# Seventeen products per context piece, five transfers for g, the selected context and v2, and an earlier Wout load

## The reference

```python
query = hidden_states @ Wq                      # 100 x 640 for each batch
keyt, valt = enc @ Wk, enc @ Wv                 # 718 x 640
hs = _mha(query, keyt, valt)                    # softmax(q k^T / sqrt(80)) v, 8 heads
ca_q1 = einsum('btc,th->bch', ca, Wq_ca)[:, indices, :]
ca_hs1 = _mha(ca_q1, residual, residual)
ca_hs2 = _mha(ca_hs1 @ Wq, ca @ Wk_ca, ca @ Wv_ca)
out = (hs + ca_hs2) @ Wout + b_out + residual
```

## Time and profile before

| what | value |
|---|---|
| three runs | 996.71, 997.91, 1003.1 us; median 997.91 |
| the profiled execution | 995.0 us, its span 993.3 us |
| granted TensorE clock, mean | 0.997 |
| busy: TensorE, VectorE, ScalarE, GpSimd | 978.8, 649.9, 489.7, 342.4 us |
| DMA | 190.12 MB, 191 GB/s |

### The profile page before, as it was taken

One profiled execution on the slowest core, in us unless ns is written; L12 is line 12 of the kernel. 1 busy time (PEld: TensorE's weight loads), 2 busy tenths in 40 slices (PEclk: granted clock), 3 DMA queues, 4 the chain that ended last, 5 costly groups with the idle time before them and its releaser, 6 DMA issues.

```text
span 993.3 us, 20727 instructions
## 1 busy us (share of the span) xinstructions
PE 978.8 (99%) x6740; PEld 959.5 (97%) x6740; DVE 649.9 (65%) x1129; ACT 489.7 (49%) x895; POOL 342.4 (34%) x286
## 2 busy tenths in 40 slices
PE   9999999999999999999999999999999999998998
PEld 8998889999999999999999999999999999997997
DVE  6455686767666666666766767676767666667444
ACT  7434546464545455454646463636364645445120
POOL 5212453333343434251616152434333333415000
PEclk9999999999999999999999999999999999999999
DMA  7899978887878787978797979697878878795364
GB/s 263 279 296 268 267 172 203 173 206 158 205 170 197 168 196 167 197 172 188 174 186 180 183 182 185 179 184 192 171 199 169 209 155 209 166 211 149 99 186 144
DMA packets 154170, 190.12 MB, mean 191 GB/s; under 512 B 80929, under 2 KB 108193, under 8 KB 154145
## 3 DMA queue, kind: packets, MB, share of 16 engines
q1 hardware_dynamic: 147456, 177.44, 76.2%
q10 hardware_dynamic: 6688, 12.35, 3.8%
HBM read 81.56 MB, written 19.95 MB: 102 GB/s over the span
## 4 chain that ended last, share of the span: by engine, by line
PE 88%; DVE 4%; DMA 3%; ACT 2%; SPq 2%; issue 1%; ACTq 0%
PE psS L744 22%; PE psB L779 20%; PE psB L784 10%; PE psS L719 8%; PE psT L760 6%; PE psS L888 6%; PE psT L806 4%; PE psT L812 2%; PE psB L923 2%; PE psS L997 1%; PE psB L861 1%; PE psB L838 1%; PE psT L813 1%; DMA encT_raw<-in_Wout_dram 1%; SPq L382 1%; PE psB L849 1%
## 5 line engine op out<-in xcount | busy, mean ns | idle before, releaser
L744 PE MATMUL psS<-encT_keep,Wk_keep 128*128 128x360 f32 x1440 | 253.8, 329 | 0.0
L744 PEld LDWEIGHTS psS<-encT_keep,Wk_keep 128*128 128x128 f32 x1440 | 237.4, 189 | 0.8
L779 PE MATMUL psB<-PT_h,encN_h 120*128 120x400 f32 x576 | 202.6, 352 | 0.0
L779 PE MATMUL psB<-PT_l,encN_h 120*128 120x400 f32 x576 | 199.0, 345 | 0.0
L1130 ACT ACTIVATE probs<-psS,negmax 100x718 f32<-100x718 f32 x128 | 110.2, 861 | 130.7 <-DVE negmax L1522 130.6
L606 POOL TENSOR_TENSOR encT_keep<-encT_raw,encT_keep 128x718 fp32r<-128x718 f32 x45 | 79.7, 1771 | 179.9 <-ACT encT_keep L1159 177.6
L1535 DVE TENSOR_TENSOR PT_l<-psT,PT_h 120x600 fp32r<-120x600 f32 x128 | 99.7, 779 | 43.3 <-ACT PT_h L1141 39.2
L614 POOL TENSOR_TENSOR encN_l<-enc_raw,encN_h 120x768 fp32r<-120x768 f32 x48 | 92.6, 1929 | 92.5 <-ACT encN_h L1166 91.1
L784 PE MATMUL psB<-PT_h,encN_l 120*128 120x400 f32 x576 | 120.4, 344 | 0.7 <-POOL encN_l L614 0.7
L597 POOL TENSOR_TENSOR Mbd<-Mbd,fmask 128x320 fp32r<-128x320 f32 x48 | 45.0, 937 | 220.6 <-DMA Mbd<-m_split 218.1
L1546 DVE TENSOR_TENSOR kT<-psS,kT 128x718 fp32r<-128x718 f32 x80 | 72.3, 903 | 69.4 <-ACT kT L1154 69.4
(11 more groups left out here) (245 smaller groups left out, 1630.1 us busy)
## 6 DMA issues: line engine op xcount, KB each, us to landing
kstack<-kT SPq DMA_DIRECT2D x64, 448.8 KB
kstack<-kT SPq DMA_DIRECT2D x192, 112.2 KB
enc_raw<-in_encN_dram SPq DMA_DIRECT2D x48, 360.0 KB, 5.5
encT_raw<-in_encT_dram SPq DMA_DIRECT2D x45, 359.0 KB, 6.2
kstack<-kT SPq DMA_DIRECT2D x32, 359.0 KB
kstack<-kT SPq DMA_DIRECT2D x32, 269.2 KB
kstack<-kT SPq DMA_DIRECT2D x32, 179.5 KB, 3.7
kstack<-kT SPq DMA_DIRECT2D x64, 89.8 KB, 3.9
```

What stands on the lines that cost most here:

```text
L744: mm = pe.matmul(keys_in(f, first)[:, half, 0:HALF], w[:, c, f * 128:(f + 1) * 128], e[:, c, k0:k0 + HALF], start=(j == 0), stop=(j == 3 * ...
L779: pe.matmul(psB[:, 1, 0:RH], eN[0][:, k, cc], PT[p][:, k, rows], start=(k == 0 and p == 0), stop=False)
```

## The change

It cuts the contraction over the keys differently. KP becomes 128: five full tiles (FULLK) hold 640 keys and the sixth holds the remaining TAIL = 78. The tail's three products become two, of 117 rows (TSTK): the rows 78 to 116 of the sixth tile hold a second half of the tail (TH = 39 rows). In eN[0] and PT[0] they hold the low part of the context's first 39 tail keys and the high part of the same keys' probabilities. In eN[1] and PT[1], rows 0 to 77 hold the context's high part again (`enc_twice`) and the probabilities' low part, and rows 78 to 116 the context's low part and the probabilities' high part of the last 39 keys. A piece is then 17 products.

The copies are made so: `norm` gets one more multiply, which writes the first 39 tail columns a second time behind column 718, so that the transposes bring them to rows 78 to 116. `tail_pt0` and `tail_pt1` move the probabilities' rows by DMA, the one from SP's queue, the other from ScalarE's. `tail_enc` moves the low part of the context in two transfers; GpSimd makes it first, in place of the raw rows, and `enc_low` becomes four instructions (1, 1, 2 and 2 key tiles, in the order 5, 4, 0-1, 2-3). The first transfer of `load_enc` brings tiles 4 and 5. Two waits are new in the last two products of a piece.

Apart from that, g comes in two transfers and not four, a in one and not two, v2 in two and not three. In the last batch Wout's load stands ahead of `lift(i, 3)`, `wo_high(2)` moves behind `u_high(i - 1, 5)`, and `enc_low` stands behind two `wo_low`, not three.

```diff
-KP = (KEYS + KT - 1) // KT
+KP = 128
 KPAD = KT * KP
-HALF = KPAD // 2
+HALF = 360
+FULLK = KEYS // KP
+TAIL = KEYS - FULLK * KP
+TH = TAIL // 2
+TSTK = TAIL + TH
...
+        tail_low = enc_raw[0:KP, FULLK * C:KT * C].bitcast(F32R)
...
+        def third(c):
+
+            return slice(4, 6) if c == 0 else slice(2 * (c - 1), 2 * c)
...
                 def load_ga(b, first=False):
                     free("gbd", b, first)
-                    for k, p in enumerate((0, 2, 0, 1)):
-                        sp.dma_start(raw(g[k * HT:(k + 1) * HT, :]), raw(g_d[p * HT:(p + 1) * HT, bass.ds(b * S, S)]))\
-                          .then_inc(s["gin"], 16)
+                    for rows, src in ((slice(0, ST), slice(0, ST)), (slice(ST, GS), slice(0, HT))):
+                        sp.dma_start(raw(g[rows, :]), raw(g_d[src, bass.ds(b * S, S)])).then_inc(s["gin"], 16)
                     free("a", b, first)
-                    a_src = asel[bass.ds(b, 1)].rearrange("o p j -> (o p) j")
-                    sp.dma_start(ar[0:ST, :], a_src).then_inc(s["ain"], 16)
-                    sp.dma_start(ar[ST:GS, :], a_src[0:HT, :]).then_inc(s["ain"], 16)
+                    a_src = asel[bass.ds(b, 1), 0:T, :].to_broadcast([GS // T, T, S])
+                    sp.dma_start(ar[:, :], a_src).then_inc(s["ain"], 16)
...
                 def load_enc(b, c, first=False):
-                    free("encN", PARTS * (b - 1) + c + 1, first)
-                    ks = slice(c * KQ, (c + 1) * KQ)
+                    free("encN", LOWS * (b - 1) + c + 2, first)
+                    if c == 0:
+                        free("entail", 32 * b, first)
+                    ks = third(c)
...
+                def tail_pt0(b):
+
+                    wait_apart(sp, s["ptlo"], HEADS * b + 4, s["passed_sp"])
+                    sp.dma_start(raw(PT[1][TAIL:TSTK, FULLK, 0:RH]), raw(PT[0][TH:TAIL, FULLK, 0:RH]))\
+                      .then_inc(s["pttail"], 16)
+
+                def tail_enc(b):
+
+                    wait_apart(sp, s["encN"], LOWS * b + 1, s["passed_sp"])
+                    for p in range(2):
+                        sp.dma_start(raw(eN[p][TAIL:TSTK, FULLK, :]), raw(tail_low[p * TH:(p + 1) * TH, :]))\
+                          .then_inc(s["entail"], 16)
+
                 def load_v2(b):
-                    for k, p in enumerate((0, 0, 1)):
-                        src = v2_d[p][bass.ds(b, 1)].to_broadcast([HEADS, T, H])
-                        sp.dma_start(raw(v2[k * HT:(k + 1) * HT, :]), raw(src)).then_inc(s["v2in"], 16)
+                    for p, rows in ((0, slice(0, 2 * HT)), (1, slice(2 * HT, ST))):
+                        src = v2_d[p][bass.ds(b, 1)].to_broadcast([(2 - p) * HEADS, T, H])
+                        sp.dma_start(raw(v2[rows, :]), raw(src)).then_inc(s["v2in"], 16)
...
+                    if last:
+                        sp.wait_ge(s["encT"], PARTS * (B - 1))
+                        load_wo(0)
                     lift(i, 3)
                     if last:
                         load_enc(i, 2)
-                        sp.wait_ge(s["encT"], PARTS * (B - 1))
-                        load_wo(0)
...
                         sp.dma_start(wv_raw, tiled(Wv)).then_inc(s["wvin"], 16)
+                    tail_pt0(i)
+                    tail_enc(i)
+                    if first:
                         load_q(i + 1)
-                    else:
+                    if not first:
                         wait_apart(sp, s["hsp"], 2 * i, s["passed_sp"])
...
                 def enc_low(b):
+                    pool.wait_ge(s["encNhi"], LOWS * b + 2)
+                    nc.gpsimd.tensor_tensor(tail_low, rawN[:, FULLK, :], eN[0][:, FULLK, :],
+                                            ALU.subtract).then_inc(s["encN"], 1)
...
+                    nc.gpsimd.tensor_tensor(eN[1][:, FULLK - 1, :], rawN[:, FULLK - 1, :], eN[0][:, FULLK - 1, :],
+                                            ALU.subtract).then_inc(s["encN"], 1)
...
-                for c in range(3):
+                for c in range(2):
                     wo_low(c)
                 enc_low(B - 1)
-                for c in range(3, FT):
+                for c in range(2, FT):
                     wo_low(c)
...
-                    for k in range(KT):
+                    for k in range(FULLK):
                         for p in range(2):
                             pe.matmul(psB[:, 1, 0:RH], eN[0][:, k, cc], PT[p][:, k, rows],
                                       start=(k == 0 and p == 0), stop=False)
-                    for k in range(KT):
-                        if u == 0 and k % KQ == 0:
-                            pe.wait_ge(s["encN"], PARTS * i + k // KQ + 1)
-                        mm = pe.matmul(psB[:, 1, 0:RH], eN[1][:, k, cc], PT[0][:, k, rows],
-                                       start=False, stop=(k == KT - 1))
-                    mm.then_inc(s["u"], 1)
+                    for n, k in enumerate((4, 0, 1, 2, 3)):
+                        if u == 0 and n in (0, 1, 3):
+                            pe.wait_ge(s["encN"], LOWS * i + (n + 1) // 2 + 2)
+                        pe.matmul(psB[:, 1, 0:RH], eN[1][:, k, cc], PT[0][:, k, rows], start=False, stop=False)
+                    if u == 0:
+                        pe.wait_ge(s["entail"], 32 * i + 32)
+                    if c == 0:
+                        pe.wait_ge(s["pttail"], 32 * i + 16 * half + 16)
+                    pe.matmul(psB[:, 1, 0:RH], eN[0][0:TSTK, FULLK, cc], PT[0][0:TSTK, FULLK, rows],
+                              start=False, stop=False)
+                    pe.matmul(psB[:, 1, 0:RH], eN[1][0:TSTK, FULLK, cc], PT[1][0:TSTK, FULLK, rows],
+                              start=False, stop=True).then_inc(s["u"], 1)
...
+                def enc_twice(b):
+
+                    nc.scalar.activation(eN[1][0:TAIL, FULLK, :], rawN[0:TAIL, FULLK, :], ACT.Copy)\
+                      .then_inc(s["encNhi"], 1)
+
+                def tail_pt1(b):
+
+                    act.wait_ge(s["ptlo"], HEADS * b + HEADS)
+                    act.dma_start(raw(PT[1][TAIL:TSTK, FULLK, RH:R]), raw(PT[0][TH:TAIL, FULLK, RH:R]))\
+                      .then_inc(s["pttail"], 16)
...
                         u_high(i - 1, 5)
+                    if last:
+                        wo_high(2)
                     pt_high(i, 3)
...
                         enc_high(i, 0)
+                        enc_twice(i)
...
-                    if not last:
+                    if last:
+                        tail_pt1(i)
+                    else:
                         u_high(i, 1)
+                        tail_pt1(i)
                         expo(i + 1, 0)
...
                     nc.vector.reciprocal(inv[:, h:h + 1], total[:, h:h + 1]).then_inc(s["inv"], 1)
-                    dve.wait_ge(s["inv"], HEADS * i + h + 1)
+                    dve.wait_ge(s["inv"], 2 * (HEADS * i + h) + 1)
+                    nc.vector.tensor_scalar(P[h % PRING][0:S, KEYS:KEYS + TH],
+                                            P[h % PRING][0:S, FULLK * KP:FULLK * KP + TH], inv[:, h:h + 1],
+                                            None, ALU.mult).then_inc(s["inv"], 1)
+                    dve.wait_ge(s["inv"], 2 * (HEADS * i + h) + 2)
                     nc.vector.tensor_scalar(P[h % PRING][0:S, 0:KEYS], P[h % PRING][0:S, 0:KEYS], inv[:, h:h + 1],
                                             None, ALU.mult).then_inc(s["norm"], 1)
```

More of the change, by code:

```diff
@@ L109, in program @@
         NP = FT + 1
+        LOWS = PARTS + 1
         HALFCOLS = slice(GT, 2 * GT)
@@ L249, in program @@
         splits = "encT encN gbd ahi a xhi xlo v2bd mbd wolo passed_sp passed_pool"
+        tails = "pttail entail"
         stage1_loads = "xT0 xT1 xT2 xT3 xT4 wqin0 wqin1 wqin2 wqin3 wqin4 wgin cain wkcain wvcain wkin encin wvin hin"
@@ L256, in program @@
         stage1_stores = "qst0 qst1 qst2 qst3a qst3b v2st mst0 mst1 mst2"
-        names = " ".join((loads, products_done, exps_and_highs, steps_and_lows, splits, stage1_loads, stage1,
+        names = " ".join((loads, products_done, exps_and_highs, steps_and_lows, splits, tails, stage1_loads, stage1,
                           stage1_stores)).split()
@@ L541, in _ @@
                 batch(B - 1, last=True)
-                sp.wait_ge(s["encN"], PARTS * B)
+                sp.wait_ge(s["encN"], LOWS * B)
                 for t in range(2):
@@ L568, in spread_g @@
                 def spread_g(b, first=False):
-                    pool.wait_ge(s["gin"], 64 * b + 64)
+                    pool.wait_ge(s["gin"], 32 * b + 32)
                     if not first:
@@ L577, in spread_g @@
                     pool.wait_ge(s["gbd"], b + 1)
-                    wait_apart(pool, s["ain"], 32 * b + 32, s["passed_pool"])
+                    wait_apart(pool, s["ain"], 16 * b + 16, s["passed_pool"])
                     nc.gpsimd.tensor_copy(As[:, :], ar[:, :]).then_inc(s["ahi"], 1)
                     pool.wait_ge(s["ahi"], b + 1)
```

(21 more changed lines are left out.)

4 lines of the change are left out of this document (2 added, 2 removed).

## The result

The changed kernel takes 993.8 us (median of ten runs, 991.1 to 995.9) against 1000.7 for ten runs of the kernel before beside it (995.8 to 1005.6). The ratio is 0.9948, with a 95% interval of 0.9930 to 0.9966: faster by 3.4 to 7.0 us, where 13 were forecast. The direction was right, the size was not, and a gain of that size is within 1%, which the prediction gave 0.32.

What follows compares the result with a forecast made beforehand. TensorE's work was taken as the bound from 131 to 890 us. 995.0 - 17.6 + 0 + 1.0 + 1.7 + 0.6 + 1.3 = 982.0, plus 2.9: 984.9 us, a gain of 13; range 979.5 to 998.

Steps and rivals of the forecast that it cites:

- Alone it is hidden: Extra multiply in each norm on VectorE: 0.2 us, eight times a batch, 1.6 us within 16 us free, mattering only through GpSimd.
- TensorE's next releasers: Two waits near TensorE in the loop: a transpose needing VectorE's result, 1.0 us, and second scores needing a lift, 1.7 us.
- The race with GpSimd: Head 3's norm: the large multiply starts 0.08 us ahead of GpSimd's next piece; taken as won, VectorE 0.3 us late.
- rival B: GpSimd's piece gets between the two multiplies every batch; large multiply over 2 us, TensorE waits on P1T; 997.8 us; chance 0.26.
- The head: First batch: the two multiplies meet the low parts of Wv, and enc_twice delays the context's low parts; 1.3 us lost (0 to 2.5).
- The rest: Last batch: Wout's earlier load gains 1.3 us, multiplies waiting for GpSimd in heads 4 to 6 lose 3; net loss taken 0.6.
- The product: Context pieces: 96 lose one product each at 0.183 us, saving 17.6 us, 1.10 us in each of 14 loop batches.
- rival C: Transposes: the eight more columns loaded cost time, giving 987.7 us, or 989.3 if the pace follows the columns; chance 0.05.
- The lift: A batch's second scores wait for a lift whose cover shrinks by 0.55 us; 1.7 us over 14 batches (0 to 7).
- The queues: SP's queue: fewer transfers save 2.1 us, three tail transfers of about 0.4 are added; ScalarE and GpSimd additions fit; cost 0.
- rival E: The last accumulation waits for a tail transfer, taking back the product's 1.10 us; no change, 998 to 1000 us; chance 0.04.
- D: GpSimd gets in twice, in the norms of heads 3 and 5, delaying exponentials and next keys; slower, 1018 us; chance 0.07.

Runs made afterwards that it cites:

- u_first: Changed kernel with u_low(i-1, 2) ahead of b2_norm's large product on VectorE, not behind it; ratio to the kernel before 0.9911.
- no_small: Changed kernel without the 39-column multiply in each norm, so half of the tail's last product is left out of the result; ratio to the kernel before 0.9859.
- small_before: Kernel before the change with only a 39-column multiply added in each norm, into a spare tile nobody reads; ratio to the kernel before 1.0102.
- both_act: Changed kernel with u_low moved ahead, the 39 columns from a small Exp, and ScalarE instead of SP issuing the three tail transfers; ratio to before 1.0053.
- queue9: Changed kernel with g, the selected context and v2 loaded by nine transfers, as before the change, in place of five; ratio to before 1.0060.
- small_last: Changed kernel with each norm's 718-column multiply first, then the 39 columns as a copy; one execution, 1004.3 us (before beside it 996.5).
- both: Changed kernel with u_low(i-1, 2) ahead of b2_norm's large product and the 39 columns from a second, small Exp; 984.6 us, ratio to before 0.9870.
- both_2: Changed kernel with u_low moved ahead and the 39 columns from a small Exp, the same kernel run again; 986.0 us, ratio to before 0.9898.
- exp_twice: Changed kernel with the 39 columns written by a second, small Exp on ScalarE and one 757-column multiply on VectorE; ratio to before 0.9907.

## Why the prediction was wrong, step by step

**The step that failed** is "1.6 us on an engine with 16 us free. Alone it is hidden", and the list under it, "TensorE's next releasers. Two come close". There is a third: the values wait for u_low(i-1, 2), which stood 0.4 to 0.5 us ahead of them, behind the norm of head 0 and b2_norm's product on VectorE. u_first and no_small each take that wait away, small_before makes it without the rest of the change: this cause is shown. The prediction put the multiply at nothing when it is alone. By the ratios it costs 9 us in the changed kernel (0.9948 less no_small's 0.9859) and 10 us in the kernel before (small_before, 1.0102), as much as the forecast's gain was off by (8).

**The size of the small multiply.** Forecast 0.2 us, measured 0.25, and 0.28 from one start to the next:

```profile
L1591 DVE TENSOR_SCALAR probs<-probs,inv 100x718 f32<-100x718 f32 x128 | 108.8, 850 | 4.5
L1587 DVE TENSOR_SCALAR probs<-probs,inv 100x39 f32<-100x39 f32 x128 | 38.1, 298 | 4.6
```

718 columns take 0.60 and 39 take 0.25, so by these two sizes an estimated 0.23 us of either is not for columns: most of the 0.25 us is fixed.

**The race with GpSimd.** At head 3, where the prediction looked for it, it was won, by the margin that it gave. It was lost at head 6, in all 14 loop batches, which the prediction did not list: there the large multiply, once 0.60, takes 2.05 to 2.07. First VectorE at both heads, then GpSimd:

```profile
527.49 0.39 DVE L1587 TENSOR_SCALAR probs<-probs,inv 100x39 f32<-100x39 f32 x1
527.91 0.60 DVE L1591 TENSOR_SCALAR probs<-probs,inv 100x718 f32<-100x718 f32 x1
...
539.22 0.24 DVE L1587 TENSOR_SCALAR probs<-probs,inv 100x39 f32<-100x39 f32 x1
539.50 2.06 DVE L1591 TENSOR_SCALAR probs<-probs,inv 100x718 f32<-100x718 f32 x1
...
527.99 2.11 POOL L635 TENSOR_TENSOR encT_keep<-encT_raw,encT_keep 128x718 fp32r<-128x718 f32 x1 [0.16 <-POOL encT_keep L635]
...
539.32 1.84 POOL L650 TENSOR_TENSOR encN_l<-enc_raw,encN_h 128x768 fp32r<-128x768 f32 x1 [1.96 <-ACT encN_h L1208]
```

This is rival B's first sign, a multiply over 2 us once a batch, without its second: TensorE has no wait on P1T, and none behind head 6. The 1.5 us are hidden, so B was not what happened.

**The head**: forecast a loss of 1.3 less three products, 0.8; the profiled pair shows 6.8. Over the traces, six kernels with the second instruction on VectorE have a head of 148.9 to 153.2 (mean 151.1), five without it 147.4 to 149.6 (mean 148.4; with both_act's 151.2 it is 148.9). So it costs 2.2 to 2.7 us there, some 2 are left for the rest of the change, and about 2 of the 6.8 are this one execution's: 18 products of keys at 132.34 took 4.76 us and not 3.21, as the granted clock fell under them (0.50 from 134 to 136 us). This division is rough. It rests on a single execution of before, and small_before, with nothing but the multiply added, has 6.1 us more than that one. In batch 0, heads 5 and 6 wait for GpSimd in both multiplies; head 6's:

```profile
124.80 1.64 DVE L1587 TENSOR_SCALAR probs<-probs,inv 100x39 f32<-100x39 f32 x1
126.48 2.23 DVE L1591 TENSOR_SCALAR probs<-probs,inv 100x718 f32<-100x718 f32 x1
```

The prediction looked at head 7 and the parts of Wv; the context's own low parts met heads 5 and 6 first. (The 2.23 is not the small multiply's doing: no_small has 2.21 there. The 1.64 is, and with it head 3's large one, 2.11 for 0.72.)

**The rest**: nine products less and a net loss of 0.6 made a gain of 1.1; measured is a loss of 1.1. Four kernels with the second instruction on VectorE and Wout's new order (after, u_first, queue9, small_last) have a rest of 118.5 to 121.0, mean 120.0; five without it 117.3 to 119.1, mean 117.8. So it takes some 2.3 us, in heads 5 and 6 again. Against it stands the gain of Wout's order, about 2. Part of the 2.3 is the clock. These are before and after:

```profile
900.00:910.00 10.00, 8.49 (x58) 7.30 (x57) 9.04 (x14) 5.33 (x12) 8.59 (x6) 1.00 0.56 156
900.00:910.00 10.00, 6.32 (x33) 4.91 (x34) 9.56 (x11) 2.94 (x6) 8.04 (x5) 0.83 0.67 194
```

TensorE stood still for 3.7 us of the latter and had part of its work at a lower granted clock (0.67 from 904 to 906 us, 0.50 from 906 to 908); u_first and queue9 show the same 0.83 at this place (queue9, whose batches are longer, from 910 to 920), small_last and no_small 1.00. What was left out is the context's first piece, whose last low products wait for GpSimd: 0.7 us before the change, 1.3 after, and 1.4 in no_small too, as TensorE comes there 2 us sooner and GpSimd's low parts take as long as before. The remainder, nearly 2 us, has no cause here; both and both_2, one kernel, differ by 1.6 in the rest.

**What held.** The product: quiet batches of both and both_2 take 50.91 to 50.96, mostly 50.93, against 51.92 to 51.95 before: 1.0 of the 1.10. The missing 0.1 shows no wait of its own. It is not the transpose behind VectorE, for which the prediction had 1.0 us: its step is 0.086 us in every loop batch, before and after, so that term came to nothing. The transposes: six at 128 columns take 0.68 us as in the earlier trace rows, while the load itself grew from 137 to 141 ns, 4 ns for eight columns, and the pace by none; rival C is out.

```profile
520.20 0.68 PE L796 MATMUL psT<-ident,probs 100*128 100x100 f32 x6
```

The lift: no wait on kstack in the changed kernel's loop, as the wait for u_low covered it; in both, exp_twice and no_small it appears, 1.0 to 1.7 us, where the sum had 1.7, and in both_2 the view has none. Late transfers may cost more than that: 14 times the mean batch less the quiet one is 1.9 us in both_2 and 3.7 to 4.8 in the other three, not all of it traced. The queues: 0 is what came out, but as the balance of two sums that are each larger than the prediction had them, and without the four transfers less it would be about 11 us. No wait on entail or pttail: rival E is out. D is out: its stalls never came. And small_last shows that B was a case to fear: with the two instructions in the other order the change took 1004.3 us.

The parts of the error, in the profiled pair: 5.5 us in the loop, 6.0 in the head, 2.2 in the rest. In the timed runs it is 8 us (a gain of 5 where 13 were forecast), as some of the head's is that execution's. How the head's other 2 us divide between enc_twice, GpSimd's extra piece and ScalarE's own issues, whose length differs from run to run, stays open.

## What to carry to other kernels

When TensorE is the bound, an engine with a third of its time free has no slack that can be read from that share: list every wait of TensorE in one period with the end of its releaser beside it, and charge any added instruction against the smallest of these covers, not against the average. Instructions of VectorE beside GpSimd's counted here by their number and not by their size, since each one may stand behind a whole piece of the other (39 columns took 1.58 us in small_last, 718 took 2.06 in the changed kernel); merge a small one into its neighbour (757 columns for 718), give it to an engine that GpSimd does not hold up (the small Exp kept its 0.29 us on ScalarE), or move the urgent result ahead of it. Where a change trades transfers for transfers on one queue, price both sides.

## What the runs showed of the hardware that was not expected

- A 39-column multiply keeps VectorE 0.25 us against 0.60 for 718 columns, a 39-column copy 0.19, a 39-column Exp on ScalarE 0.29.
- Beside a row of GpSimd pieces VectorE got one instruction in between two pieces here, and the next one waited for a whole piece, 39 columns or 718 (1.58 and 2.06 us in small_last and in the changed kernel), unless it started ahead of that piece (527.91 against 527.99 in the changed kernel: 0.60, where the one that waited took 2.06).
- Issuing a transfer of 39 rows from one tile to another held the queue for 0.75 to 0.87 us, the x load 0.40 (at 535.68 in the changed kernel).
- TensorE's granted clock fell behind some stretches with idle time, and that was part of the price of these stalls. In the last stretch below, in the head, it is 0.83 on average (0.50 from 134 to 136 us), and ten products of keys took 0.13 us longer each. The 20 us before it had TensorE busy for 16.7. In before's same stretch, behind 20 us with 20.0 busy, it is 1.00. It is no rule: in small_last TensorE was busy for 2.5 of the 5 us from 905, and the clock is 1.00 there and in the 15 us behind.

```profile
120.00:130.00 10.00, 8.44 (x53) 7.92 (x53) 9.26 (x11) 5.66 (x12) 7.08 (x6) 1.00 0.55 154
130.00:140.00 10.00, 8.75 (x48) 8.43 (x49) 6.79 (x17) 5.47 (x11) 5.60 (x6) 0.83 0.60 136
```
